# A decoder layer with experts: the output bias matmul over 128 rows with zeros instead of 64 rows

## The reference

```
x = x + attn(layernorm(x))
x = x + memory_attn(layernorm(x), ctx_2048, mask)
h = layernorm(x)
logits = h @ router.T + router_bias;  top-2, softmax over the two -> scores[t, e]
gate_up = h @ gate_up_proj[e] + gate_up_proj_bias[e]
gate = min(gate, 7);  up = clip(up, -7, 7)
act = (up + 1) * gate * sigmoid(1.702 * gate)
expert_out[e] = act @ down_proj[e] + down_proj_bias[e]
out = x + sum over e of scores[t, e] * expert_out[e]
```

## Time and profile before

| | us |
|---|---|
| median of 3 runs | 1690.19 |
| lowest and highest | 1689.7, 1690.42 |
| the profiled execution | 1693.16 |
| its span, first to last instruction | 1691.4 |
| TensorE busy in it | 1532.3 (91%) |
| VectorE busy | 1383.5 (82%) |
| ScalarE busy | 1115.8 (66%) |
| GpSimd busy | 1047.6 (62%) |

### The profile page before, as it was taken

The page is one execution under the profiler, slowest core; times in us unless marked ns, Lnnn a source line. Parts: engine busy times, 40 slices in busy tenths (PEclk is TensorE's granted clock), DMA queues, the critical chain, the costliest instruction groups (busy, mean ns, idle before and its releaser), DMA issues. The chain is left out here.

```text
span 1691.4 us, 31714 instructions
## 1 busy us (share of the span) xinstructions
PE 1532.3 (91%) x8951; PEld 1324.5 (78%) x8951; DVE 1383.5 (82%) x3470; ACT 1115.8 (66%) x2593; POOL 1047.6 (62%) x1161
## 2 busy tenths in 40 slices
PE   5799999999999999999999998699499999999994
PEld 4687877887787787887777877498388888888883
DVE  7898888898898898898898887477588888888882
ACT  3788878778777877787777877322165555555651
POOL 6589779789679779779769866546522233222321
PEclk9999999999999999999999999755599999999997
DMA  4000000000000000000000000112468778877765
GB/s 169 1 14 20 1 14 20 1 13 19 1 13 19 1 13 19 1 13 19 1 13 0 1 1 1 40 69 88 166 177 226 219 208 215 230 220 208 191 169 131
DMA packets 62002, 124.47 MB, mean 74 GB/s; under 512 B 20942, under 2 KB 21070, under 8 KB 61792
## 3 DMA queue, kind: packets, MB, share of 16 engines
q1 hardware_dynamic: 51408, 102.24, 18.8%
q0 software_dynamic: 10304, 20.59, 6.7%
q10 hardware_dynamic: 144, 0.07, 0.0%
HBM read 106.08 MB, written 24.71 MB: 77 GB/s over the span
## 5 line engine op out<-in xcount | busy, mean ns | idle before, releaser
L522 POOL TENSOR_SCALAR probs<-probs,row_inv 128x512 f32<-128x512 f32 (+3 forms) x512 | 280.6, 567 | 25.6 <-DVE row_inv L426 25.6
L306 ACT ACTIVATE probs<-probs,neg_max 128x512 f32<-128x512 f32 (+3 forms) x512 | 281.5, 552 | 10.5 <-DVE neg_max L419 6.8
L419 DVE CUSTOM_DVE_ANT_0 probs<-bank,causal 128x512 f32<-128x512 f32 (+3 forms) x512 | 220.6, 485 | 57.3 <-PE bank L208 43.8
L1209 POOL DMA_INDIRECT acc<-ctx_raw,idx x46 | 74.5, 1619 | 311.0 <-ACT ctx_raw L1362 300.5
L218 PE MATMUL bank<-ident,probs 128*128 128x128 f32 x1280 | 187.4, 277 | 53.6 <-POOL probs L522 35.7
L407 DVE TENSOR_TENSOR pt_lo<-bank,pt_hi 128x512 fp32r<-128x512 f32 (+1 forms) x384 | 214.9, 586 | 22.8 <-ACT pt_hi L299 22.7
L218 PEld LDWEIGHTS bank<-ident,probs 128*128 128x128 f32 x1280 | 150.3, 142 | 101.0 <-issue 45.7
L513 POOL TENSOR_TENSOR rot<-rot,sin 128x512 f32<-128x512 f32 (+1 forms) x96 | 123.9, 1291 | 166.0 <-DVE rot L438 162.5
L1290 PE MATMUL bank<-xt_hi,gu_hi 128*128 128x256 f32 x736 | 208.0, 283 | 1.5 <-DVE xt_lo L407 1.5
L1290 PE MATMUL bank<-xt_hi,gu_lo 128*128 128x256 f32 x736 | 206.4, 280 | 0.0
L1290 PE MATMUL bank<-xt_lo,gu_hi 128*128 128x256 f32 x736 | 206.2, 280 | 0.0
(11 more groups left out here) (204 smaller groups left out, 4209.2 us busy)
## 6 DMA issues: line engine op xcount, KB each, us to landing
gu_raw<-in_gate_up SPq DMA_DIRECT2D x92, 512.0 KB, 3.7
dn_raw<-in_down SPq DMA_DIRECT2D x92, 256.0 KB, 3.6
w_raw<-in_wqkv SPq DMA_DIRECT2D x8, 768.0 KB, 4.5
w_raw<-in_wo_rows SPq DMA_DIRECT2D x8, 512.0 KB, 3.5
h_rows<-ln_h SPq DMA_DIRECT2D x16, 256.0 KB, 2.0
acc<-x_res SPq DMA_DIRECT2D x4, 1024.0 KB, 4.6
x_res<-in_x SPq DMA_DIRECT2D x3, 1024.0 KB, 11.2
ctx_raw<-in_ctx SPq DMA_DIRECT2D x2, 512.0 KB, 6.8
```

The lines of the kernel that those rows point to most:

```text
L306: nc.scalar.activation(row, row, ACT.Exp, bias=neg_max[:, hb, i:i + 1], scale=-1.0, accum_out=row_sum[:, hb, i:i + 1]).then_inc(s["exp_don ...
L419: nc.vector.tensor_tensor_reduce(out=probs[:, hb, P_AT[i]:P_AT[i] + (i + 1) * P], in0=S_BANK[k][:, at:at + (i + 1) * P], in1=causal[:, (QB ...
L522: nc.gpsimd.tensor_scalar(row, row, row_inv[:, hb, i:i + 1], 0.0, ALU.mult, ALU.add).then_inc(s["pnorm_done"], 1)
```

## The change

The buffers `expert_row`, `down_raw`, `down_bias` and `expert_hot` get 128 rows instead of 64, and the bias matmul takes all 128. Rows 64 to 127 of `down_bias` are zero since GpSimd clears `down_raw` in full, and those of `expert_hot` are zero since their row number is no expert's. The work on the setup, as lines 1546, 1551, 1454 and 1137, covers the whole buffers and so 128 rows as well; lines 1554 and 1517 are as before.

```
-        expert_row = st("expert_row", [2 * 32, 1])
+        expert_row = st("expert_row", [P, 1])
...
-        down_raw = st("down_raw", [2 * 32, D])
-        down_bias = st("down_bias", [2 * 32, D], F32R)
-        expert_hot = st("expert_hot", [2 * 32, NT], F32R)
+        down_raw = st("down_raw", [P, D])
+        down_bias = st("down_bias", [P, D], F32R)
+        expert_hot = st("expert_hot", [P, NT], F32R)
...
-            nc.vector.tensor_scalar(expert_hot[:, :], tile_e[0:2 * 32, :], expert_row[:, 0:1], None, ALU.is_equal).then_inc(z["hot_done"], 1)
+            nc.vector.tensor_scalar(expert_hot[:, :], tile_e[:, :], expert_row[:, 0:1], None, ALU.is_equal).then_inc(z["hot_done"], 1)
...
-                    nc.tensor.matmul(Y_BANK[n % 3][:, :], expert_hot[:, tau:tau + 1].to_broadcast([2 * 32, P]), down_bias[:, :], start=True, stop=False)
+                    nc.tensor.matmul(Y_BANK[n % 3][:, :], expert_hot[:, tau:tau + 1].to_broadcast([P, P]), down_bias[:, :], start=True, stop=False)
```

## The result

The changed kernel takes 1676.75 us (median of 6 runs, 1673.25 to 1680.39) where the kernel before, run beside it, takes 1690.66 us. The ratio is 0.991, 95% interval 0.9896 to 0.9925, which is 15.2 us of 1690.66 (12.7 to 17.6). The forecast was 1673.0 us, a ratio of 0.9898.

What follows compares the result with a forecast made beforehand. TensorE, without idle time in the expert stage, was taken as the bound. 23 tiles x 0.75 = 17.25 us, less 0.05 for the tail, gave 17.2: 1690.19 - 17.2 = 1673.0 us, range 1669.6 to 1679.

Steps and rivals of the forecast that it cites:

- TensorE sets the end of the expert stage: Expert stage: TensorE has no real idle time, 428.92 of 429.00 us busy, so time it saves shortens the kernel.
- 0.75 us per tile: TensorE, expert stage: a tile's stretch around its two bias matmuls falls from 2.75 to 2.00 us with 128 rows.
- All 23 tiles: Expert stage: the full 0.75 us is gained in every tile, 23 x 0.75 = 17.25 us.
- VectorE's floor 385.9 us: Expert stage: VectorE could give up its 43.1 us of waiting for TensorE, 429 - 43.1, against TensorE's new 411.75.
- The tail: Last tile's GpSimd scatter also waits for earlier scatters to land; 0 to 0.75 us lost, 0.05 written off.
- The setup at nothing: Clearing and rounding the bias buffer and the expert tables cost nothing on more partitions; 1.1 us if doubled without cover.
- the 0.9 us I gave it: Expert stage: cover left between ScalarE's row scalings and the second bias matmul that needs the freed bank.
- rival 3: Expert stage: TensorE's clock drops once per tile, costing 39 us, so 1712 us; chance 0.03.
- Rivals 1 and 2: Bias matmul: pauses not from its rows, no effect, 1690.2 us, chance 0.05; or half the gain, 1681.6, chance 0.05.
- single clock drops in attention: Attention stage: one short TensorE clock drop more or less, 1.7 us each, counted in the forecast's spread.
- the spread I gave for it: Whole kernel: 1671 to 1676.5 us, from the tail's 0.7, setup up to 1.1 and one clock drop, 1.7.
- rival 2: Expert stage: new bias matmul costs about halfway, 0.42 us, or a follower is late; half the gain, 1681.6 us; chance 0.05.

Runs made afterwards that it cites:

- the setup alone: Changed kernel with its 128-row buffers, but the bias matmul reads rows 0 to 63: 1692.6 us beside 1693.13 for the kernel before, ratio 0.9999.
- the two comparisons: Changed kernel, unedited, measured twice against the kernel before: 1676.75 us beside 1690.66 (ratio 0.991), then 1675.14 beside 1693.13 (ratio 0.9896).

## Why the prediction was right, point by point

**TensorE sets the end of the expert stage.** Right, and the count of 64-row matmuls shows it: 0, 1 and 2 matmuls of 64 rows per tile give periods of 18.26, 18.66 and 19.04 us, and the distance from first to last bias matmul follows. It would not have stayed right for much more, as the kernel without bias matmuls shows.

**0.75 us per tile.** Measured 0.78 (19.04 - 18.26). The term was mis-sized by 0.03, since the 128-row steps are 0.11 and 0.23 there, and not 0.12 and 0.235.

**All 23 tiles.** Wrong for the first and the last. Tile 0's period fell by 0.17 us only, from 19.90 to 19.73; in the other profiles it is 19.86 to 19.91 us with two 64-row matmuls apart and 19.52 to 19.85 with none. The changed kernel there, a TensorE weight load and VectorE:

```profile
1243.48 0.19 PEld L1290 LDWEIGHTS bank<-xt_hi,gu_hi 128*128 128x128 f32 x1 [0.88 <-issue]
```

```profile
1242.12 1.29 DVE L407 TENSOR_TENSOR xt_lo<-bank,xt_hi 128x512 fp32r<-128x512 f32 x2 [0.55 <-ACT xt_hi L299]
```

VectorE, after 0.55 us of waiting for ScalarE, ends the rows' low part at 1243.41, and TensorE waits for it (line 1290 starts at 1243.51): the wait that the kernel without bias matmuls has in every tile. I had called VectorE's floor 385.9 us for the stage, by taking all its time behind the wait for line 1290 as free. This was the faulty step, though it cost the forecast little: the idle time of VectorE isn't free to close up in this order of work. By an estimate from the kernel without bias matmuls, 22 tiles at 18.05 us are 397 us.

**The tail.** I left the last tile's gain in doubt between 0 and 0.75 us and wrote off 0.05; it was lost. GpSimd's last scatters in the changed kernel, and ScalarE's last row scalings:

```profile
1643.84 1.58 POOL L1209 DMA_INDIRECT acc<-ctx_raw,idx  x1 [3.60 <-issue]
1649.36 1.57 POOL L1209 DMA_INDIRECT acc<-ctx_raw,idx  x1 [3.93 <-DMA acc<-ctx_raw,idx]
```

```profile
1646.85 1.30 ACT L1362 ACTIVATE ctx_raw<-bank,sh 128x512 f32<-128x512 f32 x2 [1.63 <-PE bank L1310]
```

The scaling ends at 1648.15 and the scatter starts 1.21 us later, where it started 0.28 later before: its releaser is now the landing of the scatter ahead, no longer ScalarE. The reading of which wait comes next was right, its share in the sum too small: what lies behind the last bias matmul grew by 0.4 us.

**The rest.** The setup at nothing: shown by the setup alone. ScalarE's scalings and the weight transfers never made TensorE wait in an inner tile; the bank of the second bias matmul needs only the first of the two scalings (`n - 2`), so its cover was larger than the 0.9 us I gave it. The clock stayed at 1.00, so rival 3 had nothing to stand on. Rivals 1 and 2 fall with the period. In sum 17.2 us were forecast for the stage with its tail, and the profile has 17.2 - 0.4 = 16.8; the two comparisons, 15.2 and 17.6 us, lie on both sides. The median of 1676.75 us lies 3.75 us above the forecast's 1673.0, and the expert stage accounts for only some 0.4 us of that. The rest belongs to the movement ahead of it, which I had put at 0.2% and at single clock drops in attention; the measured median lies just above the spread I gave for it (1671 to 1676.5), and the range held it because I had widened it towards rival 2, a third of the gain lost, which did not come about. That part was luck.

## What to carry to other kernels

In this stream of 128-row matmuls, each one of 64 or 32 rows cost a round trip of 0.39 us on top of the time for its columns; look for it by start times and by a weight load that no longer starts with the matmul ahead. Fill the operands with zero rows, pack two halves into one, or put such matmuls side by side. Before counting such a gain in every tile, find the wait that comes next (here VectorE's low part with 0.2 us of cover, and the last scatter's landing), since idle time of an engine with a fixed order is not all cover.

## What was not expected of the hardware

The number of rows does not set the price by itself: 96 rows pass like 128, without a pause, while 32 rows cost as much as 64. And the time from kernel start to the expert stage moves by some 6 us between executions with the same instructions there; the granted clock of the memory stage was between 0.52 and 0.58 in them, and did not account for it.
